# Neighbourhood attention: the gate's two layers, the spread of the inverse row sums, and the order in which the input is loaded

## The reference

```
qkv = (x @ qkv_w + qkv_b)            # 4 heads of 32; q scaled by 32 ** -0.5
kwin, vwin = 7 x 7 neighbourhood of each pixel, clamped at the borders
scores = einsum(q, kwin) + bias      # bias by relative place, 49 scores a pixel and head
attn = softmax(scores)
out = einsum(attn, vwin) @ proj_w + proj_b
gate = sigmoid(relu(x @ g1_w + g1_b) @ g2_w + g2_b)   # g1_w 128 x 64, g2_w 64 x 1
x1 = out * gate + x
```

## Time and profile before

| | before |
|---|---|
| median of three runs | 4184.15 us |
| the profiled execution's own time | 4181.7 us |
| its span (first to last instruction) | 4179.6 us |
| mean granted TensorE clock | 0.941 |
| busy: PE / PEld / DVE / ACT / POOL | 94 / 72 / 76 / 66 / 29% |
| first layer | from 0 to about 655 us |

### The profile page before, as it was taken

How to read it: one execution, slowest core, us unless ns; L and a number is a source line. 1 busy time by engine, 2 the same in 40 slices (tenths; PEclk the granted TensorE clock), 3 DMA queues, 4 the chain that set the end, 5 groups by cost and what they waited for, 6 DMA issues and landing times. The chain is left out here.

```text
span 4179.6 us, 73566 instructions
## 1 busy us (share of the span) xinstructions
PE 3919.2 (94%) x25466; PEld 3010.7 (72%) x25466; DVE 3167.0 (76%) x7667; ACT 2743.9 (66%) x6175; POOL 1220.1 (29%) x1283
## 2 busy tenths in 40 slices
PE   7999997999999999999999999978899977889899
PEld 5777775899888998899988999955566643333347
DVE  5888886777777777777777777769466668887775
ACT  4777775677776777767777666659343457766643
POOL 2444543000020000200002000034134458887753
PEclk8999998999999999999999999999899976778789
DMA  6766651000010000100001000032243335554446
GB/s 181 187 176 172 177 161 41 17 22 23 14 49 19 26 19 21 41 23 22 23 17 44 9 11 9 9 95 84 91 143 135 130 127 178 172 166 155 144 156 212
DMA packets 284588, 365.84 MB, mean 88 GB/s; under 512 B 38842, under 2 KB 169914, under 8 KB 283450
## 3 DMA queue, kind: packets, MB, share of 16 engines
q1 hardware_dynamic: 270346, 343.83, 27.1%
q0 software_dynamic: 12288, 16.92, 1.5%
q10 hardware_dynamic: 1584, 0.40, 0.1%
HBM read 192.80 MB, written 115.34 MB: 74 GB/s over the span
## 5 line engine op out<-in xcount | busy, mean ns | idle before, releaser
L917 ACT ACTIVATE l_ph<-l_T 128x512 fp32r<-128x512 f32 x1024 | 611.7, 597 | 549.7 <-PE l_T L822 549.7
L1034 DVE TENSOR_TENSOR l_pl<-l_T,l_ph 128x512 fp32r<-128x512 f32 x1024 | 707.6, 691 | 274.8 <-ACT l_ph L917 274.1
L1023 DVE CUSTOM_DVE_ANT_0 l_pr<-l_S,l_zero 128x512 f32<-128x512 f32 x1024 | 705.0, 689 | 74.8 <-PE l_S L745 11.9
L922 ACT ACTIVATE l_pr<-l_pr,l_st 128x512 f32<-128x512 f32 x1024 | 731.6, 715 | 1.1 <-DVE l_st L1029 1.0
L834 PE MATMUL l_O<-l_ph,l_vh 128*128 128x256 f32 x2048 | 661.6, 323 | 12.3 <-DVE l_pl L1034 12.1
L822 PE MATMUL l_T<-l_ident,l_pr 128*128 128x128 f32 x4096 | 613.2, 272 | 0.0
L822 PEld LDWEIGHTS l_T<-l_ident,l_pr 128*128 128x128 f32 x4096 | 508.0, 140 | 136.5 <-issue 0.2
L835 PE MATMUL l_O<-l_ph,l_vl 128*128 128x256 f32 x2048 | 577.9, 282 | 0.0
L836 PE MATMUL l_O<-l_pl,l_vh 128*128 128x256 f32 x2048 | 576.9, 282 | 0.0
L1066 POOL TENSOR_TENSOR l_xs<-l_xs,l_bob 128x128 f32<-128x128 f32 x128 | 57.3, 460 | 1644.0 <-DMA l_xs<-x 1642.6
L743 PE MATMUL l_S<-l_kh,l_qh 128*128 128x512 f32 x1024 | 416.9, 407 | 0.3 <-DVE l_kl L983 0.2
(11 more groups left out here) (259 smaller groups left out, 8138.3 us busy)
## 6 DMA issues: line engine op xcount, KB each, us to landing
l3b_u<-ub SPq DMA_DIRECT2D x128, 512.0 KB, 3.9
l_kq<-l_hl SPq DMA_DIRECT2D x372, 128.0 KB, 3.3
zs<-l_tmp SPq DMA_DIRECT2D x64, 256.0 KB, 2.2
ub<-l3a_u SPq DMA_DIRECT2D x32, 512.0 KB, 3.1
l3b_z<-zs SPq DMA_DIRECT2D x64, 256.0 KB, 3.6
yz<-l3b_z SPq DMA_DIRECT2D x64, 256.0 KB, 3.3
l3b_dt<-yz SPq DMA_DIRECT2D x32, 512.0 KB, 4.1
l_vg<-vs SPq DMA_DIRECT2D x256, 55.0 KB
```

What stands on the lines that cost most here:

```text
L917: e.activation(ph[:, i, :], psT[:, i, :], ACT.Copy).then_inc(p_hi, 1)
L922: e.activation(pr[:, s, es], pr[:, s, es], ACT.Exp, bias=st[:, s, 9:10], scale=SC, accum_out=st[:, s, 10 + k:11 + k]).then_inc(exped, 1)
L1023: e.tensor_tensor_reduce(pr[:, s, ks], psS[:, bk, :], zero[:].broadcast_to([128, 512]), 1.0, -3.0e38, ALU.add, ALU.max, st[:, s, kc:kc + 1 ...
L1034: e.tensor_tensor(pl[:, i, :], psT[:, i, :], f32(ph[:, i, :]), ALU.subtract).then_inc(p_lo, 1)
```

## The change

It has three parts.

1. The gate. The first layer takes 128 pixels as weights four times and lets the 64 columns of g1_w stream past, so that its output has pixels on partitions (128 x 4 x 64). VectorE adds the bias out of the bank, applies the relu and multiplies by g2_w in one instruction, and reduces over the 64 columns to four numbers a pixel partition. ScalarE's exponential reads those. The second layer's products on TensorE and the relu on ScalarE are gone, at the start of the stage too.
2. The inverse row sums. `invert` writes each inverse 32 times, into `rx` (128x128, two slots), from a source that repeats each sum; one product with the identity turns it into the 128x128 spread in place of the four side by side.
3. The input. The kernel gets x a second time, `xB`, with the pixels of a block together. q and hide read it from `xq`, k and v read `xn`; each has two slots, where `xn` had three. The ring for x on GpSimd has six slots, where it had seven. At the start two rows are fetched in both orders ahead of the constants, and row 2 behind the stacks of rows 0 and 1.

```diff
-        g2w = P.sb("g2w", [64, 1])
+        g1b, g2w = P.sb("g1b", [128, 64]), P.sb("g2w", [128, 64])
...
-        xn = P.sb("xn", [128, 3, 512])
+        xn = P.sb("xn", [128, 2, 512])
+        xq = P.sb("xq", [128, 2, 512])
...
-        gt = P.sb("gt", [64, 512])
+        gt = P.sb("gt", [128, 256])
...
-        st = P.sb("st", [128, 4, 16])
+        st = P.sb("st", [128, 4, 12])
+        rx = P.sb("rx", [128, 2, 128])
...
-        xs = P.sb("xs", [128, 7, 128])
+        xs = P.sb("xs", [128, 6, 128])
...
-            def fetch(G):
+            def fetch_rows(G):
                 b, rb = divmod(G, 8)
-                s, sl = G % 3, slice(512 * rb, 512 * rb + 512)
-                if G >= 3:
-                    for what in ("k", "q", "v", "hide"):
-                        full(w, (what, G - 3))
-                e.dma_start(xn[:, s, :], io["xT"][b, :, sl]).then_inc(xn_in[s], 16)
+                if G >= 2:
+                    for what in ("k", "v"):
+                        full(w, (what, G - 2))
+                e.dma_start(xn[:, G % 2, :], io["xT"][b, :, 512 * rb:512 * rb + 512]).then_inc(xn_in[G % 2], 16)
+
+            def fetch_blocks(G):
+                b, rb = divmod(G, 8)
+                if G >= 2:
+                    for what in ("q", "hide"):
+                        full(w, (what, G - 2))
+                e.dma_start(xq[:, G % 2, :], io["xB"][b, :, 512 * rb:512 * rb + 512]).then_inc(xq_in[G % 2], 16)
 
...
-            for G in range(3):
-                fetch(G)
-            for dst, src in ((bvb[:], row(io["L0_conv_qkv_b"], 256, 384)), (g1w[:], io["L0_conv_g1_w"]), (g2w[:], io["L0_conv_g2_w"]),
-                             (cols[0:64, 3:4], col(io["L0_conv_g1_b"])), (cols[:, 4:5], row(io["L0_conv_g2_b"], 0, 1)),
+            for G in range(2):
+                fetch_rows(G)
+                fetch_blocks(G)
+            for dst, src in ((bvb[:], row(io["L0_conv_qkv_b"], 256, 384)), (g1w[:], io["L0_conv_g1_w"]), (g2w[:], row(io["L0_conv_g2_w"].rearrange("a b -> (a b)"), 0, 64)),
+                             (g1b[:], row(io["L0_conv_g1_b"], 0, 64)), (cols[:, 4:5], row(io["L0_conv_g2_b"], 0, 1)),
                              (ident[:], io["ident"]), (wp[:], io["L0_conv_proj_w"]), (pbb[:], row(io["L0_conv_proj_b"], 0, 128))):
                 e.dma_start(dst, src, allow_slow_non_contiguous=True).then_inc(weights, 16)
             bias(0)
             stack(0)
             stack(1, ("k",))
+            fetch_rows(2)
+            fetch_blocks(2)
             keep_v(0)
             keep_v(1)
             stack(1, ("q",), q1_in)
-            fetch(3)
+            fetch_rows(3)
+            fetch_blocks(3)
             bias(1)
             bring(0)
             bias(2)
...
                     elif what == "v":
                         keep_v(G)
+                        if G + 2 < NB:
+                            fetch_rows(G + 2)
                     elif what == "hide" and G + 2 < NB:
-                        fetch(G + 2)
+                        fetch_blocks(G + 2)
...
-                if n >= 7:
-                    w.wait_ge(y_done, n - 6)
-                e.dma_start(xs[:, n % 7, :], io["x"][b, r0:r0 + 8, c0:c0 + 16, :]).then_inc(xs_in[n % 7], 16)
+                if n >= 6:
+                    w.wait_ge(y_done, n - 5)
+                e.dma_start(xs[:, n % 6, :], io["x"][b, r0:r0 + 8, c0:c0 + 16, :]).then_inc(xs_in[n % 6], 16)
...
             def project(what, G):
-                s = G % 3
+                s = G % 2
...
-                if what in ("q", "k"):
-                    w.wait_ge(xn_in[s], 16 * (G // 3 + 1))
+                if what in ("q", "hide"):
+                    w.wait_ge(xq_in[s], 16 * (G // 2 + 1))
+                else:
+                    w.wait_ge(xn_in[s], 16 * (G // 2 + 1))
+                if what == "q":
                     w.wait_ge(prepared, 3)
-                    if what == "q":
-                        e.matmul(bank, wqkv[:, 0:128], blocks(xn[:, s, :]), start=True, stop=True).then_inc(done, 1)
-                    else:
-                        e.matmul(bank, wqkv[:, 128:256], xn[:, s, :], start=True, stop=True).then_inc(done, 1)
+                    e.matmul(bank, wqkv[:, 0:128], xq[:, s, :], start=True, stop=True).then_inc(done, 1)
+                elif what == "k":
+                    w.wait_ge(first, 32)
+                    e.matmul(bank, wqkv[:, 128:256], xn[:, s, :], start=True, stop=True).then_inc(done, 1)
                 elif what == "v":
-                    w.wait_ge(xn_in[s], 16 * (G // 3 + 1))
                     w.wait_ge(first, 32)
                     for k in range(4):
                         t = e.matmul(bank[:, 128 * k:128 * k + 128], xn[:, s, 128 * k:128 * k + 128], wqkv[:, 256:384], start=True, stop=True)
                     t.then_inc(done, 1)
-                elif what == "hide":
-                    w.wait_ge(xn_in[s], 16 * (G // 3 + 1))
+                else:
                     w.wait_ge(weights, 128)
-                    e.matmul(bank[0:64, :], g1w[:], blocks(xn[:, s, :]), start=True, stop=True).then_inc(done, 1)
-                else:
-                    w.wait_ge(P_free, p_use["hide", G] + 1)
                     for k in range(4):
-                        t = e.matmul(bank[:, k:k + 1], gt[:, 128 * k:128 * k + 128], g2w[:], start=True, stop=True)
+                        t = e.matmul(bank[:, 64 * k:64 * k + 64], xq[:, s, 128 * k:128 * k + 128], g1w[:], start=True, stop=True)
                     t.then_inc(done, 1)
...
-                G = opening(n + 2) if h == 0 else None
-                if G is not None:
-                    w.wait_ge(P_free, p_use["hide", G] + 1)
-                    for k in range(4):
-                        e.matmul(psT[:, 0, 384 + k:385 + k], gt[:, 128 * k:128 * k + 128], g2w[:], start=True, stop=True)
...
             for what, G in before:
-                project(what, G)
+                if what != "open":
+                    project(what, G)
...
                     w.wait_ge(summed, n - 2)
                     if n >= 4:
                         w.wait_ge(y_done, n - 3)
-                    for h in range(4):
-                        t = e.matmul(psF[32 * h:32 * h + 32, 0:128], st[:, (n - 3) % 4, 12 + h:13 + h].broadcast_to([128, 32]), ident[:],
-                                     start=True, stop=True, tile_position=(0, 32 * h))
-                    t.then_inc(R_full, 1)
+                    e.matmul(psF[:, 0:128], rx[:, (n - 3) % 2, :], ident[:], start=True, stop=True).then_inc(R_full, 1)
...
-                elif what == "hide":
-                    full(w, (what, G))
+                elif what == "open":
                     w.wait_ge(prepared, 4)
-                    e.activation(gt[:], psP[0:64, :], ACT.Relu, bias=cols[0:64, 3:4]).then_inc(P_free, 1)
-                elif what == "open":
-                    full(w, (what, G))
-                    e.activation(gate[:, 0, 4 * G:4 * G + 4], psP[:, 0:4], ACT.Exp, bias=cols[:, 4:5], scale=-1.0).then_inc(P_free, 1)
+                    w.wait_ge(opening_in, G + 1)
+                    e.activation(gate[:, 0, 4 * G:4 * G + 4], gate[:, 0, 4 * G:4 * G + 4], ACT.Exp, bias=cols[:, 4:5], scale=-1.0).then_inc(opened_out, 1)
...
                         G = opening(n) if h == 0 else None
                         if G is not None:
-                            e.activation(gate[:, 0, 4 * G:4 * G + 4], psT[:, 0, 384:388], ACT.Exp, bias=cols[:, 4:5], scale=-1.0).then_inc(opened_out, 1)
+                            project("open", G)
                         e.activation(ptb[0:110, n % 2, h, :], psT[0:110, 0, 0:384], ACT.Copy).then_inc(T_even, 1)
...
+                elif what == "hide":
+                    t, per = gt[:].rearrange("p (k c) -> p k c", k=4), lambda v: v.rearrange("p (a c) -> p a c", a=1).broadcast_to([128, 4, 64])
+                    full(w, (what, G))
+                    w.wait_ge(weights, 128)
+                    e.tensor_tensor(t, bank[:, 0:256].rearrange("p (k c) -> p k c", k=4), per(g1b[:]), ALU.add).then_inc(free, 1)
+                    w.wait_ge(P_free, p_use[what, G] + 1)
+                    e.scalar_tensor_tensor(t, t, 0.0, per(g2w[:]), ALU.max, ALU.mult).then_inc(weighted, 1)
+                    w.wait_ge(weighted, G + 1)
+                    e.tensor_reduce(gate[:, 0, 4 * G:4 * G + 4], t, AX.X, ALU.add).then_inc(opening_in, 1)
                 elif what == "open":
                     sl = slice(4 * G, 4 * G + 4)
-                    if G < 2:
-                        emptied(w, (what, G))
-                    else:
-                        w.wait_ge(opened_out, G - 1)
+                    w.wait_ge(opened_out, G + 1)
                     e.tensor_scalar(gate[:, 1, sl], gate[:, 0, sl], 1.0, None, ALU.add).then_inc(gate_den, 1)
                     w.wait_ge(gate_den, G + 1)
                     e.reciprocal(gate[:, 2, sl], gate[:, 1, sl]).then_inc(gated, 1)
...
             def invert(n):
```

(20 more changed lines are left out.)

5 lines of the change are left out of this document (3 added, 2 removed).

## The result

The changed kernel took 4207.48 us (median of 4, 4201.86 to 4211.02), the kernel before 4180.06 us in the same comparison (4 runs): a ratio of 1.0064, with an interval of 1.0045 to 1.0083. It is 27 us slower. Other runs come with their ratio to the kernel before, measured beside it, and the interval. The profiled executions are 4201.86 us (span 4200.1) and 4181.7 us (span 4179.6); what follows compares these two.

What follows compares the result with a forecast made beforehand. TensorE bounds the kernel; after the change VectorE would, at 15.85 + 2.11 + 1.30 = 19.26 us a row. Rows 20.7, last blocks 4.8, start 3: +28.5 us, median 4211; own range 4191 to 4225, wider 4166 to 4262.

Steps and rivals of the forecast that it cites:

- The inverse: VectorE, each block: 128x128 where it was 128x4, 4.25 ns an element, 0.53 us more a block, 2.11 a row.
- VectorE's base: VectorE's existing work a row, without the change's new parts: 15.85 us of each 18.52.
- The gate, 1.30: VectorE, once a row: three instructions (bias add, relu with product, reduction) cost 1.30 us; bounds 1.05 to 1.5.
- TensorE: 0.4 us too low: TensorE's row after the change: 18.52 − 0.98 − 0.40 − 0.04 = 17.1 us.
- The 0.40 that I had taken off for the single product: TensorE's spread of inverse row sums: one product takes 0.23 us where four took 0.33, −0.40 us a row.
- TensorE sets the pace: Kernel before: TensorE, busy 99.23 of 100 us, bounds the rows; VectorE is 16% away from doing so.
- the row of 18.52: Baseline row of four blocks, between key projections at 399.96 and 418.48; the change was to lengthen it by 0.74 us.
- Input in two orders: I count nothing: Sync queue: one more transfer a row at some 0.4 us, 17.35 becoming 17.75 us, adds nothing to the row.
- hidden under 19.26 and not hidden under 17.1: Sync queue's 17.75 us a row fits within VectorE's predicted row of 19.26 but exceeds TensorE's 17.1.
- The start: 3 predicted: Stage start: extra fetches ahead of the second bias table make it about 3 us late; bounds 0 and 6.
- The tail: 4.8 predicted: Last nine blocks, without jobs: VectorE runs them without a gap, 9 x 0.53 = 4.8 us more.
- the inverse streams: VectorE: 128 elements cost 1.04 ns each beyond the fixed part, row about 17.9 us, kernel 4169 us; chance 0.16.

Runs made afterwards that it cites:

- The ruler: Kernel before with reciprocals of 4 to 512 elements, contiguous or from repeated sources, timed in its prologue; 6.25 ns an element; kernel time not read.
- the small inverse and four products: Changed kernel with the 128x4 inverse and four 32-column products restored, gate and both input orders kept; 4201.95 us, ratio 1.0050.
- GpSimd's repeats: Changed kernel with a 128x4 inverse on VectorE, GpSimd copying each column 32 times into the 128x128 tile, one product; 4196.3 us, ratio 1.0032.

## Why the prediction was right, and where it was not

The forecast was slower, 4211 us by the inverse on VectorE; it came to 4207. The mechanism is there: VectorE at 98.79%, the others waiting for it, rows of 19.38 us where I had 19.26. Behind that agreement stand errors that cancel, and one step that failed. And the mechanism is not the whole of it: the wide inverse makes VectorE the bound, but with it gone late stacking transfers hold the rows as long. The second transfer is a part of that (0.30 us a row) and not all of it: without both, in two kernels, the mean rows are 19.21 and 18.91, far over the 17.5 that TensorE needs.

*The inverse: mis-sized.* I had 0.53 us more a block from a slope of 4.25 ns an element; it is 0.77 (0.86 for 0.09). The slope came from two rows with 4 and 16 elements in different stages, 173 and 224 ns. The ruler has 178 and 253 for these sizes in one place, hence 6.25. Twelve elements are too short a base: my rows lay 5 and 29 ns below it, and those 24 ns of difference were a third of the slope. The Trainium skill (VectorE: DVE Perf Modes, section "First, the fixed hardware budget") gave 8.3 ns an element as I read its repeat count, an estimate; the measured 6.25 lies between it and mine.

*VectorE's base: too large.* I had 15.85 us a row. The measured row less its new parts, 19.38 − 4 x 0.77 − 1.24, leaves 15.06. The block that I measured had no idle time noted, but TensorE's pace was in it: from score to score 0.48 there, 0.40 in the changed kernel. This error is 0.8 us a row, the inverse's 1.0 the other way.

*The gate, 1.30: right* (1.24; 410, 425 and 420 ns for 414, 476 and 410). The relu with product did not cost more than the others.

*TensorE: 0.4 us too low.* I had 17.1 us; the shortest rows are 17.49 with the small inverse and four products, and 17.50 with GpSimd's repeats and one. The 0.40 that I had taken off for the single product is the difference: it did not go to 0.23, it holds TensorE from 383.65 to 383.98, 0.33 us as the four did. The first layer holds it for 0.81, not 0.96 (0.91 with the four products), which by itself should have made the row shorter still; why the row shows nothing of that was not followed up.

*"TensorE sets the pace" and the row of 18.52: wrong as a baseline.* I took one row of the shortest kind. The mean is 19.03. So the change cost 0.44 us a row, not 0.74, and 11.0 us over the rows, not 20.7. One row is a poor sample where rows differ; the rows' whole series would have shown it at once, and also that two were over 20. That the total agrees is in part luck: I had 25.5 us for the rows and the last blocks, where 11.4 were measured, and the idle time behind the stage, the later stages and a median that rose by 7 us more than the profiled execution, none of them foreseen, made up for it.

*"Input in two orders: I count nothing": the step that failed.* I had the sync queue at 17.35 us of a row of 18.52, and 17.75 with the second transfer. The 17.35 were the groups of one cycle without the gaps between them, and that cycle itself ran 18.88 us, to the group at 401.28. With the gaps the queue is occupied for 18.24 us of a mean cycle of 18.98; with the second transfer, 19.2 of 19.4. My own sentence, hidden under 19.26 and not hidden under 17.1, had the right form and the wrong number. In the changed kernel the wide inverse hides it, so the total did not show the error; the run with the two orders alone did, with 18 us.

*The start: 3 predicted,* 3.9 at the second table, 3.3 by block 8. *The tail: 4.8 predicted,* 3.5 for the end of the stage, mostly from idle time between the stages, which I had not foreseen and cannot explain.

*The median* rose by 27 us, the profiled execution by 20.5. The stages behind, with the same code in every kernel, took 3517 to 3530 us in fourteen profiled executions, so some microseconds of either sum are not the change's. Whether the changed kernel adds some there stays open.

*The rival "the inverse streams"* was priced at 4169, as if a cheap inverse made the kernel faster. The runs with the small inverse, 4202 and 4196 us, show that it would not have.

## What to carry to other kernels

Before you credit a saving on the bound engine, measure the next floors from means over many rows, the issuing queue among them; a queue that is occupied for 18.2 us in a row of 19.0 has little left, and one more transfer is not free. Sum it issue by issue, since a merged row can hide a wait; and look at when the transfers land, since taking one off the queue did not help where the landings grew later. When removing the suspect gives nothing back, look for a second limit of the same height, and test the two parts alone. And keep a per-element price to rows that span the size in question: a spread by repeated inverse was cheaper here as a small inverse and a copy on an engine that has time (4196 us against 4207, and 4183 against 4201 without the second transfer).

## What the runs showed of the hardware

- A reciprocal on VectorE costs 6.25 ns an element, 178 ns at 4 and 3353 ns at 512, whether its source is contiguous or one column read again and again.
- An issue on the sync queue costs 0.29 us for 4 bytes, 0.35 to 0.47 for a 128x512 input, 0.60 for a stacking transfer and 0.70 for a value transfer at the median; 20 of 547 took over 0.9 us, up to 1.9, in the kernel before from 200 to 600 us, and the other kernels have such issues too.
- With input transfers issued by GpSimd the others landed later: with one a row, stacking transfers after 4.0 us and not 3.3 at the median (kernel before); with two, after 4.9 and not 3.5 (changed kernel, small inverse). The cause was not found.
- TensorE idle for 2.26 us was followed by a granted clock of 0.58 over the next 4 us, idle for 1.22 us in the kernel before (at 366.7) by the lower level from 367.8 to 371.2; but 2.14 us of idle time, with the small inverse, was not. In the changed kernel, idle in pieces of at most 0.55 us, 4.7 us in 100, it stayed at 1.00.
